# Reordering VectorE in the pair layer and lagging the attention layer by three groups in a four-layer graph network

## The reference

```python
# layer 2 ("pair"): for every edge, summed by source node
h = relu(concat(node[src], node[dst]) @ W1 + b1)
interaction = h @ W2 + b2
gated = interaction * sigmoid(interaction @ Wg + bg)
pooled = segment_sum(gated, src) / count
# layer 3 ("attention"): four heads of 16 features, softmax over the edges of a destination
g = leaky_relu(xl[src] + xr[dst] + edge_attr @ W_e, 0.2)
logits = einsum(g, att)
amax = segment_max(logits, dst)
ex = exp(logits - amax[dst])
out = segment_sum(xl[src] * ex / segment_sum(ex, dst)[dst], dst) + bias
```

## Time and profile before

| | us |
|---|---|
| median of 3 runs | 6530.24 |
| lowest, highest | 6523.35, 6541.23 |
| the profiled execution's own time | 6528.89 |
| its span, first to last instruction | 6527.2 |
| PE busy | 3615.7 (55%) |
| DVE busy | 3719.8 (57%) |
| POOL busy | 3543.2 (54%) |
| ACT busy | 1769.3 (27%) |
| PE's mean granted clock | 0.68 of full |

### The profile page before, as it was taken

How to read it: one execution, slowest core, us unless ns; L and a number is a source line. 1 busy time by engine, 2 the same in 40 slices (tenths; PEclk the granted TensorE clock), 3 DMA queues, 4 the chain that set the end, 5 groups by cost and what they waited for, 6 DMA issues and landing times. The chain is left out here.

```text
span 6527.2 us, 58257 instructions
## 1 busy us (share of the span) xinstructions
PE 3615.7 (55%) x12150; PEld 2056.4 (32%) x12150; DVE 3719.8 (57%) x4301; ACT 1769.3 (27%) x3305; POOL 3543.2 (54%) x3662
## 2 busy tenths in 40 slices
PE   3565656573444544444444434676767667677662
PEld 2344434331222222222222212333333333333331
DVE  9978955552333333333333333777777777777776
ACT  1233323361111111111111111333333333333332
POOL 4430033326666666666666656666666666666653
PEclk8566667675666666666776655767676776766765
DMA  8756467613343344333333312333333333333331
GB/s 195 205 188 201 150 159 199 108 30 88 98 101 101 101 100 101 102 101 100 100 102 99 101 41 62 84 86 83 87 85 85 85 85 86 85 87 84 86 82 32
DMA packets 1376052, 678.01 MB, mean 104 GB/s; under 512 B 1051533, under 2 KB 1254927, under 8 KB 1374994
## 3 DMA queue, kind: packets, MB, share of 16 engines
q1 hardware_dynamic: 1099684, 341.45, 22.5%
q0 software_dynamic: 116880, 124.33, 10.0%
q10 hardware_dynamic: 159390, 211.24, 9.4%
HBM read 344.06 MB, written 332.55 MB: 104 GB/s over the span
## 5 line engine op out<-in xcount | busy, mean ns | idle before, releaser
L1650 POOL DMA_INDIRECT got<-tabg,ix x1568 | 1483.1, 946 | 892.8 <-DMA t<-rows 442.4
L1456 POOL DMA_INDIRECT got<-tabg,ix x1568 | 1483.0, 946 | 825.1 <-issue 436.7
L1476 PE MATMUL p_inter<-hid,W 128*128 128x512 f32 x392 | 388.9, 1094 | 1230.7 <-DVE run L1562 1031.5
L1554 DVE TENSOR_TENSOR_SCAN own<-mk,own,p_first 128x512 f32<-128x512 bf16 x195 | 248.8, 1276 | 1426.7 <-remote 762.7
L177 PE MATMUL p_out<-ident,run 128*128 128x128 f32 (+1 forms) x3136 | 688.5, 369 | 171.8 <-DVE run L493 66.3
L177 PEld LDWEIGHTS p_out<-ident,run 128*128 128x128 f32 (+1 forms) x3136 | 572.2, 218 | 531.7 <-issue 416.4
L1785 DVE TENSOR_TENSOR_SCAN top<-p_reset,top,logit 128x512 f32<-128x512 f32 x195 | 249.5, 1280 | 575.4 <-DMA tops<-top 263.2
L163 PE MATMUL p_small<-ident,ea 128*32 128x128 f32 (+1 forms) x784 | 176.1, 370 | 712.9 <-ACT rows L1748 660.4
L1476 PEld LDWEIGHTS p_inter<-hid,W 128*128 128x128 f32 x392 | 95.4, 302 | 1274.6 <-issue 1108.9
L1508 ACT ACTIVATE gate<-p_gate,BF 128x512 f32<-128x512 f32 x196 | 134.8, 688 | 1059.7 <-issue 807.8
L493 DVE TENSOR_TENSOR_SCAN run<-p_mk,run,feat 128x512 f32<-128x512 f32 x302 | 370.4, 1268 | 63.5 <-remote 42.0
(11 more groups left out here) (347 smaller groups left out, 6749.5 us busy)
## 6 DMA issues: line engine op xcount, KB each, us to landing
t<-rows ACTq DMA_DIRECT2D x195, 512.0 KB
first<-start SPq DMA_DIRECT2D x780, 128.0 KB
t<-rows ACTq DMA_DIRECT2D x195, 288.0 KB
got<-tabg,ix POOLq DMA_INDIRECT x3136
start<-zeros SPq DMA_DIRECT2D x100, 500.0 KB
ea<-in_ea_dram SPq DMA_DIRECT2D x390, 128.0 KB
mk<-marks SPq DMA_DIRECT2D x780, 64.0 KB
start<-zeros SPq DMA_DIRECT2D x195, 256.0 KB
```

The lines of the kernel that those rows point to most:

```text
L1456: nc.gpsimd.indirect_dma_start(got[s][0:g.p, cc, h, :], None, tabg, bass.IndirectOffsetOnAxis(ap=ix[0:g.p, g.n, h, cc:cc + 1], axis=0)).th ...
L1476: nc.tensor.matmul(p_inter[s][:, 0:g.w], W2[:, :], hid[s][:, 0:g.w], start=True, stop=True).then_inc(mixed, 1)
L1650: nc.gpsimd.indirect_dma_start(got[s][0:g.p, cc, h, :], None, tabg, bass.IndirectOffsetOnAxis(ap=ix[0:g.p, g.n, h, cc:cc + 1], axis=0)).th ...
```

## The change

In the pair layer DVE's list is put in another order: the two steps on the old group stand first in a tick. In the attention layer the softmax steps run three groups behind instead of two, and turning back four instead of three; the running maxima lie in four tiles instead of two; the reset marks are loaded in a step and under a semaphore of their own, one tick later than the other loads, whose waits change; and `den` is turned back by four ordinary matmuls with eight columns of the identity as moving operand (one column in sixteen), instead of four full 128x128 turns. The attention stage also writes 12 of its first ticks out singly instead of 7.

```diff
-                each(dve, (0, spread), (1, add), (4, multiply), (4, accumulate))
+                each(dve, (4, multiply), (4, accumulate), (0, spread), (1, add))
...
-    R = 2 * HEADS
+    R, TOPS = 2 * HEADS, 4
...
-        top = [sb(c, f"top{i}", [P, 1 + W]) for i in range(2)]
+        top = [sb(c, f"top{i}", [P, 1 + W]) for i in range(TOPS)]
...
+        def each(eng, *steps):
+            run_ticks(eng, 0, NG + 1 + max(lag for lag, _ in steps), steps, 3 * AHEAD)
...
                 def load(g):
                     s, row = g.slot(AHEAD), snapped(sp, g.row)
-                    wait_from(sp, resets, g.n - AHEAD + 1)
                     wait_from(sp, owned, g.n - AHEAD + 1)
+                    wait_from(sp, turned_ea, g.n - AHEAD + 1)
...
-                    sp.dma_start(rs[s][:, 0:g.w], marks[0][:, 1, ds(row, g.w)]).then_inc(first_in[s], 16)
+
+                def load_resets(g):
+                    s = g.slot(AHEAD)
+                    wait_from(sp, resets, g.n - AHEAD + 1)
+                    sp.dma_start(rs[s][:, 0:g.w], marks[0][:, 1, ds(snapped(sp, g.row), g.w)]).then_inc(rs_in[s], 16)
...
-                each_group(sp, (0, load), (5, store_top))
+                each(sp, (0, load), (1, load_resets), (6, store_top))
...
-                    wait_from(pe, drained_small, g.n - 2)
+                    wait_from(pe, drained_small, g.n - 3)
...
-                    turn_to_edges(nc, p_small[:, :].rearrange("p (c q) -> p c q", c=C), den[g.slot(2)], g, ident).then_inc(smalls, 1)
+                    for cc in range(C):
+                        mm = nc.tensor.matmul(p_small[0:g.p, cc * R:(cc + 1) * R], by_place(den[g.slot(2)], g)[:, :, cc], ident[:, 0:P:HC], start=True, stop=True)
+                    mm.then_inc(smalls, 1)
...
-                each_group(pe, (2, score), (1, add_edge_terms), (0, first_rows), (3, turn_back), (3, small_back), (0, gathered_rows), (0, edge_rows))
+                each(pe, (3, score), (1, add_edge_terms), (0, first_rows), (4, turn_back), (4, small_back), (0, gathered_rows), (0, edge_rows))
...
-                each_group(act, (2, exps), (1, fifths), (3, to_rows), (3, store), (0, their_rows), (0, edge_rows), (1, keep_logits))
+                each(act, (3, exps), (1, fifths), (4, to_rows), (4, store), (0, their_rows), (0, edge_rows), (2, keep_logits))
...
-                    s = g.slot(2)
-                    wait_from(dve, tops_out[s], 16 * g.turn(2))
+                    s, m = g.slot(2), g.slot(TOPS)
+                    wait_from(dve, tops_out[m], 16 * g.turn(TOPS))
...
-                each_group(dve, (2, maximum), (2, exponents), (1, attend), (0, spread), (1, leak), (2, accumulate))
+                each(dve, (3, maximum), (3, exponents), (1, attend), (0, spread), (1, leak), (3, accumulate))
```

More of the change, by code:

```diff
@@ L1598, in edges_4 @@
         zeroed, made, weights_in = (sem(c, n) for n in ("zeroed", "made", "weights_in"))
-        first_in, got_in, mk_in = ([sem(c, f"{n}{i}") for i in range(AHEAD)] for n in ("first_in", "got_in", "mk_in"))
-        stored, tops_out = ([sem(c, f"{n}{i}") for i in range(2)] for n in ("stored", "tops_out"))
+        first_in, got_in, mk_in, rs_in = ([sem(c, f"{n}{i}") for i in range(AHEAD)] for n in ("first_in", "got_in", "mk_in", "rs_in"))
+        stored = [sem(c, f"stored{i}") for i in range(2)]
+        tops_out = [sem(c, f"tops_out{i}") for i in range(TOPS)]
         (resets, turned_first, turned_ea, turned_got, featured, gotten, summed_ea, owned, added, leaked, scored,
@@ L1622, in load @@
                         sp.dma_start(mk[s][h * D:(h + 1) * D, 0:g.w], marks[0][h, 0:1, ds(row, g.w)].to_broadcast((D, g.w))).then_inc(mk_in[s], 16)
[L1623 removed]
+                def load_resets(g):
+                    s = g.slot(AHEAD)
+                    wait_from(sp, resets, g.n - AHEAD + 1)
+                    sp.dma_start(rs[s][:, 0:g.w], marks[0][:, 1, ds(snapped(sp, g.row), g.w)]).then_inc(rs_in[s], 16)
                 def store_top(g):
[L1627 removed]
+                    s = g.slot(TOPS)
                     sp.wait_ge(maxed, g.n + 1)
                     sp.dma_start(tops[:, ds(snapped(sp, g.row), g.w)], top[s][0:P:HC, 1:1 + g.w]).then_inc(tops_out[s], 16)
[L1631 to L1633 removed]
+                each(sp, (0, load), (1, load_resets), (6, store_top))
+                for s in range(TOPS):
+                    sp.wait_ge(tops_out[s], 16 * ((NG + TOPS - s) // TOPS))
             @block.gpsimd
@@ L1667, in first_rows @@
                     s = g.slot(AHEAD)
-                    pe.wait_ge(first_in[s], 80 * g.turn(AHEAD) + 80)
+                    pe.wait_ge(first_in[s], 64 * g.turn(AHEAD) + 64)
                     wait_from(pe, owned, g.n)
@@ L1734, in exps @@
                         wait_from(act, lefts, g.n)
-                        nc.scalar.activation(top[1 - s][:, 0:1], top[s][:, W:W + 1], ACT.Copy).then_inc(carried, 1)
+                        nc.scalar.activation(top[(g.base + 1) % TOPS][:, 0:1], top[g.slot(TOPS)][:, W:W + 1], ACT.Copy).then_inc(carried, 1)
                     act.wait_ge(falls, g.n + 1)
@@ L1746, in to_rows @@
                     act.wait_ge(smalls, g.n + 1)
-                    small = p_small[0:g.p, :].rearrange("p (c h a f) -> p c h a f", h=2, a=HEADS, f=HC)
+                    small = p_small[0:g.p, 0:C * R].rearrange("p (c h a) -> p c h a", h=2, a=HEADS)
                     nc.scalar.activation(rows[s][0:g.p, :, :, D:D + HEADS].rearrange("p h c f -> p c h f"),
-                                         small[:, :, :, :, 0], ACT.Copy).then_inc(drained_small, 1)
+                                         small, ACT.Copy).then_inc(drained_small, 1)
                 def store(g):
```

20 lines of the change are left out of this document (9 added, 11 removed).

## The result

The changed kernel takes 6553.01 us (median of 7 runs, 6540.54 to 6560.42) against 6527.24 us (7 runs) for the kernel before: ratio 1.0036, 95% interval [1.0026, 1.0046]. Two later comparisons gave 1.0015 [1.0004, 1.0026] (before 6493.26 us) and 1.0015 [1.0003, 1.0027] (before 6485.59 us). The forecast was 6527 us. The time lies in the range, but it is slower by more than the noise, where no change was forecast.

A forecast was written before the change was run, and what follows sets the result against it. POOL's gathers (9.98 us per group) plus pauses for PE's late signals were taken as the bound. Terms -4 - 4 + 6 = -2 us on 6528.9 gave 6527 us; range 6395 to 6590, from the terms' near bounds 6500 to 6555.

The forecast's parts named there:

- a debt per group: Both stages: gathering runs up 1.4 to 1.9 us per group, paid in POOL's pauses, however these are spread.
- The wait for `run`: Pair stage: PE's 3.59 us wait for DVE's scan before `p_inter` goes, but POOL stays the limit.
- that for the maxima's store: Attention stage: DVE's `top` no longer waits for the store, up to 88 us of DVE's time; 0 us taken.
- The lag: Attention stage: 0 us while gathering (-65 to +41); one more round of softmax work behind the last gather, +6 us.
- the three rivals: Pauses vanish (6401 us, chance 0.20); maxima store was the bound (6441, 0.08); one pause per group (6572 to 6607, 0.21).
- one per group: Rival, pair stage: each pause frees one buffer only, +43 or +78 us; 0.21 together with other lengthened pauses.
- the maxima's wait: Rival, attention stage: the store of the maxima was the bound, so -88 us, 6441 us; chance 0.08.
- the signs named: Right if groups stay 11.6-11.9 and 12.0-12.3 us apart, pauses 300-350 and 400-430 us, and ACT starts 2.2 us after a gather.
- so it is hidden: 0 us: Attention stage: eight-column turns add 0 to +1.4 us on PE, covered by PE's 4.9 us of standing.
- the 0 for the lag, the tiles and the loads: Attention stage while gathering: lag 0 us (-65 to +41), four maxima tiles 0, loads 0 (-20 to +20).
- -4 from a range of -8 to +14: Pair stage gathers: the new order changes pauses from 1.72 to 1.68-1.79 us per group over 196 groups.
- -4 us, four or five groups at 1 us each: Behind the pair stage's last gather: the remaining groups' 9.33 us loop is free, 1 us saved each.

The follow-up runs named there:

- eight buffers: Kernel before with eight gathered-row buffers instead of four in the pair stage, plus the lag, four tiles and separate load in attention: ratio 1.0088, pair stage 11.71 us per group.
- the fillers: Kernel before with POOL filling an unread tile twice per group in the attention stage, and SP's pair-stage loop DMAs issued by ACT: ratio 0.9934.

## Why the prediction was right and wrong

**Right, and shown:** on chips with pauses the period is set by POOL and a debt per group that hardly depends on how pauses are spread (in the pair stage half as many pauses and eight buffers, in the attention stage the fillers alone). The wait for `run` went, and the pair stage got no shorter; that for the maxima's store went, and the attention stage got no shorter. What the four tiles do alone wasn't tried. The lag costs one round behind the last gather: +6 forecast, +6.0 measured (+6.9 where nothing pauses, 151.5 against 144.6). The eight matmuls cost PE 1.27 us more in the tick shown, within the bound of +1.4 (1.1 us on average); the lower granted clock, which no term had, brings another 0.5 us per group. ACT starts 2.0 us after a gather's end, as in the kernel before. None of the three rivals came: the pair stage has fewer and longer pauses that add up to the same, not one per group, and the maxima's wait gave nothing. Of the signs named, one missed by little: the attention stage's pauses are 434 us, beyond the 400 to 430.

**Wrong:** the step "so it is hidden: 0 us" for the eight-column turns, and the 0 for the lag, the tiles and the loads. I took POOL's 12.12 us as a cover under which PE's and SP's work is free. Only 9.98 of it is POOL; the other 2.12 is pauses, and they grew with both edits: 8.8 and 12.2 us in all, 0.05 and 0.06 us per group. Where POOL has no pauses, the same two edits left the stage at 1958.5 us, so POOL's own 9.98 us is a full cover and the leak is in the pauses. It is a small leak: PE's work grew by over 300 us, and 8.8 came through. Whether the pauses grew because more of PE's signals or of its work fall into them isn't shown. Both terms lie inside the bounds that I gave. In the pair stage I took -4 from a range of -8 to +14, whose middle is +3, and +6.9 and +8.2 came. (Small slips in the sum: 414 us over 195.9 groups are 2.11, not 2.12 us, and 1.94 - 1.72 is 0.22 in one place and 0.21 in another. They move nothing.) That the total lies 26 us from the forecast, and no further, is in part luck: 27 us more in the gathers against 19 less between the stages, and up to 10 that may not be the change's.

**Mis-sized:** behind the pair layer's last gather I took -4 us, four or five groups at 1 us each. It gave 14.6 to 19.3 us on chips with pauses, some 4 us per group, and 2 to 3 in all on the others, where the signals are prompt and PE is nearly through when the gathers end. This gain hid most of what the gathers lost.

**Not settled:** how PE's signals and POOL's descriptors come to be in each other's way. It takes POOL's gathers (behind the last one the signals are prompt), it is a matter of the chip, and moving SP's DMAs to ACT takes a little off. Which part makes the pauses grow inside "the lag with the loads" (the lag, the four tiles, the separate load, the changed waits) wasn't tried apart. The Trainium skill ("Perfetto Trace Analysis", section "Tensor Engine Instruction (MATMUL, LD_WEIGHTS)") says that a matmul's shown end is an estimate and its signal follows PSUM's acknowledgement. That alone doesn't give the 5 to 7 us: on a chip without pauses DVE starts 0.10 us behind the shown end.

## What to carry to other kernels

A wait of the critical engine is a weaker cover than its own work: ask what the wait pays for, and whether what you put under it makes the price go up. Here most of the work was hidden and a few per cent came through. A part of the time between two stages is the backlog of the last groups, and a quicker loop gives there what it can't give in the steady part. Before explaining a wait that no instruction ends, look at the same program on another chip.

## What the hardware showed that I had not expected

- The same kernel takes 6486 to 6533 us on some chips and 5559 to 5564 us on others. The gathers themselves are as long on both (944 to 947 ns); on the first sort what waits for PE's signals goes on 5 to 7 us after the work in the ticks read here (4319.7 to 4324.91, 2811.7 to 2818.57) while POOL gathers, on the other 0.1 us after the matmul's end.
- On the first sort POOL could do 381 us of other work in a stage at about no cost in time: 12.01 us per group with two fillers of 0.97 us, against some 12.0 estimated for the kernel before on that chip (12.12 and 12.13 in its traces elsewhere). On the other sort they cost 1.69 us per group, 10.00 to 11.69.
- Two issues of a plain DMA on SP, with the register instructions between them, take up to 4.4 us in the kernel before where POOL pauses (median 1.42), and 1.33 us where it doesn't; ACT's have a median of 1.34 us on both. The same DMAs issued by ACT in the pair stage make the period 0.2 us shorter (11.73 to 11.49).
- A transpose of 128x128 fp32 is cheap: four take 0.64 us at full clock, while four ordinary fp32 matmuls with only eight columns show as eight and take 1.92 us. Over the attention stage that is 140.6 against 355.9 us, and with them the stage's granted clock is 0.65 to 0.66, without them 0.70 to 0.71 (chips with pauses).
